# A Mamba block with its convolutions on one core: extras in other state slots, convolutions in five parts, other states' products on GpSimd

## What is computed

```python
x = x + _L0_conv_ref(_gn(x))      # 3x3 dilation (max)
x = x + _L1_conv_ref(_gn(x), ...) # pixel-unshuffle by 4, LayerNorm, Mamba, shuffle back
x = x + _L2_conv_ref(_gn(x), ...) # 3x3 convolution, 8 -> 8 channels
x = x + _L3_conv_ref(_gn(x), ...) # the same with other weights
```

```python
h = h * jnp.exp(dt_t[..., None] * A) + (dt_t * x_t)[..., None] * B_t[:, None, :]
y = jnp.einsum('bds,bs->bd', h, C_t)
```

## Time and profile before

| what | value |
|---|---|
| time, median of 3 runs | 15,045.57 us (15,040.47 to 15,050.49) |
| the profiled execution | 15,054.33 us, its span 15,052.5 us |
| VectorE busy | 13,978.7 us, 93% |
| POOL busy | 13,580.6 us, 90% |
| TensorE busy | 12,595.5 us, 84% |
| ScalarE busy | 8,975.3 us, 60% |
| chain that ended last, by engine | PE 33%, DVE 29%, issue 21%, POOL 9%, ACT 4% |
| TensorE's mean granted clock | 0.949 |

### The profile page before, as it was taken

One profiled execution on the slowest core, in us unless ns is written; L12 is line 12 of the kernel. 1 busy time (PEld: TensorE's weight loads), 2 busy tenths in 40 slices (PEclk: granted clock), 3 DMA queues, 4 the chain that ended last, 5 costly groups with the idle time before them and its releaser, 6 DMA issues.

```text
span 15052.5 us, 162697 instructions
## 1 busy us (share of the span) xinstructions
PE 12595.5 (84%) x27626; PEld 4973.4 (33%) x27626; DVE 13978.7 (93%) x12371; ACT 8975.3 (60%) x16239; POOL 13580.6 (90%) x6103
## 2 busy tenths in 40 slices
PE   4888888888888888888888888888888888888887
PEld 1333333333333333333333333333333333333332
DVE  5999999999999999999999999999999999999995
ACT  3556665566665666665656665666656666666563
POOL 5999999999999999999999999999999999999995
PEclk9999999999999999999999999999999999999998
DMA  3343443434434344443444434344343444434442
GB/s 93 105 118 116 111 123 104 125 108 112 123 106 127 106 111 121 111 124 104 113 121 110 123 106 121 113 112 122 105 129 105 109 123 111 122 107 113 121 109 81
DMA packets 1258399, 1701.57 MB, mean 113 GB/s; under 512 B 402204, under 2 KB 551140, under 8 KB 1257124
## 3 DMA queue, kind: packets, MB, share of 16 engines
q1 hardware_dynamic: 1257220, 1689.56, 40.4%
HBM read 1525.54 MB, written 124.13 MB: 110 GB/s over the span
## 4 chain that ended last, share of the span: by engine, by line
PE 33%; DVE 29%; issue 21%; POOL 9%; ACT 4%; DVEq 1%; DMA 1%; SPq 1%; POOLq 0%; ACTq 0%
PE y_ps L1026 18%; DVE h L1192 16%; DVE u_in L1176 10%; POOL hc L659 7%; PE side_ps L1037 2%; PE side_ps L1041 2%; PE b_ps L1077 2%; PE proj_ps L980 2%; POOL u_in L636 2%; PE y_ps L1023 2%; PE proj_ps L1002 2%; PE side_ps L1012 1%; PE side_ps L1045 1%; DVE vmax L1155 1%; DVE stats L1124 1%
## 5 line engine op out<-in xcount | busy, mean ns | idle before, releaser
L659 POOL TENSOR_TENSOR hc<-h,c_sb 128x1024 f32<-128x1024 f32 x4096 | 9604.5, 2358 | 952.5 <-DVE h L1192 816.6
L1192 DVE TENSOR_TENSOR_SCAN h<-a_ps,carry,u_in 128x512 f32<-128x512 f32 x7168 | 8774.5, 1264 | 367.0 <-ACT a_ps L792 196.1
L1026 PE MATMUL y_ps<-hc,ident 128*128 128x512 f32 x16400 | 8183.7, 629 | 446.3 <-POOL hc L659 440.0
L792 ACT ACTIVATE a_ps<-dt,a_neg 128x512 f32<-128x512 f32 x8192 | 5569.3, 688 | 4634.2 <-DVE h L1192 4604.4
L1026 PEld LDWEIGHTS y_ps<-hc,ident 128*128 128x128 f32 x16400 | 3191.3, 200 | 3985.2 <-issue 3065.3
L1176 DVE TENSOR_TENSOR u_in<-dtx,b_ps 128x1024 f32<-128x1024 f32 x2816 | 3368.2, 1196 | 228.0 <-PE b_ps L1077 186.4
L636 POOL TENSOR_TENSOR u_in<-dtx,b_sb 128x1024 f32<-128x1024 f32 x1281 | 3020.9, 2358 | 0.1
L1077 PE MATMUL b_ps<-b_parts,select 96*128 96x512 bf16 x2816 | 1123.9, 399 | 1639.7 <-DVE u_in L1176 1594.1
L1077 PEld LDWEIGHTS b_ps<-b_parts,select 96*128 96x128 bf16 x2816 | 278.5, 99 | 3169.7 <-DVE u_in L1176 2599.2
L1192 DVE TENSOR_TENSOR_SCAN h<-a_ps,u_in 128x512 f32<-128x512 f32 x1024 | 1202.5, 1204 | 69.0 <-POOL hc L659 55.8
L980 PE MATMUL proj_ps<-u_ln,w_x 128*128 128x512 f32 x2064 | 971.8, 593 | 4.6 <-ACT u_ln L744 3.7
(11 more groups left out here) (100 smaller groups left out, 7224.3 us busy)
## 6 DMA issues: line engine op xcount, KB each, us to landing
c_sb<-bc_dram SPq DMA_DIRECT2D x4100, 256.0 KB, 3.2
b_sb<-bc_dram SPq DMA_DIRECT2D x1283, 256.0 KB, 3.2
raw<-x SPq DMA_DIRECT2D x68, 512.0 KB
x_dram<-vmax SPq DMA_DIRECT2D x68, 512.0 KB, 4.6
z<-x_dram SPq DMA_DIRECT2D x68, 512.0 KB, 8.8
out<-raw SPq DMA_DIRECT2D x272, 128.0 KB
x_dram<-x SPq DMA_DIRECT2D x129, 256.0 KB, 4.0
x<-x_dram SPq DMA_DIRECT2D x136, 224.0 KB, 8.3
```

Of the source, the lines that this page charges most:

```text
L659: pool.tensor_tensor(hc[:, ring_at(c * S + s, HC_RING)], h[:, ring_at(c * S + s, H_RING)], c_sb[:, s // C_GROUP % C_RING, s % C_GROUP:s % ...
L792: act.activation(a_ps[:, a_slot(c * S + s, half)], dt[:, c % 2, half], ACT.Exp, scale=a_neg[:, at:at + 1]).then_inc(a_made, 1)
L1026: mm = pe.matmul(y_ps[:, half], ident[:, :], hc[:, ring_at((c * S + s) % (NC * S), HC_RING), half], start=False, stop=(s == S - 1), skip_g ...
L1192: dve.tensor_tensor_scan(h[:, r, half], a_ps[:, a_slot(c * S + s, half)], u_in[:, s % U_RING, half], start, ALU.mult, ALU.add).then_inc(h_ ...
```

## The change

Ten of the 32 states stay with POOL, but state 22 and 25 go to VectorE, and 0 and 24 to POOL. The last matmul of the output projection moves from slot 5 to slot 8, and ScalarE's copy of it (`RESIDUAL`) from 5 to 7, SP's store with it. ScalarE's copies of the x projection move from slots 6 and 9 to 7 and 10, the Silu block from 13 to 14, the base of the next chunk from 10 to 12, the softplus inputs from 20 and 22 to 21 and 23. Each convolution is issued in five parts instead of four (identity and edge were one part), in the slots of `PLACES`. The group norm "z1" is one slot later.

```diff
-POOL_U = [2, 6, 9, 11, 14, 17, 19, 22, 25, 27]
+POOL_U = [0, 2, 6, 9, 11, 14, 17, 19, 24, 27]
...
-CENTER, VAR, OUT = 0, 3, 5
+CENTER, VAR, OUT = 0, 3, (5, 5, 8)
...
-COPY_X, COPY_Z, SILU = (6, 9), (11, 13), 13
-GATE, STORE_X2, BASE = 2, OUT + 1, 10
+COPY_X, COPY_Z, SILU, RESIDUAL = (7, 10), (11, 13), 14, 7
+GATE, STORE_X2, BASE = 2, RESIDUAL + 1, 12
...
-SPLUS_IN, SOFTPLUS, SUM_DT, DT_X, NEXT_G1 = (20, 22), 23, (23, 24), (25, 27), 30
-PLACES = ((15, 16, 19, 22), (24, 25, 26, 27), (28, 30, S + 2, S + 2))
+SPLUS_IN, SOFTPLUS, SUM_DT, DT_X, NEXT_G1 = (21, 23), 23, (23, 24), (25, 27), 30
+PLACES = ((15, 16, 18, 19, 22), (24, 25, 26, 27, 28), (29, 30, 31, S + 1, S + 2))
...
-MEAN_AT = {"joint": (0, 23), "z1": (3, 29), "x1": (6, 24)}
-VAR_AT = {"joint": (0, 26), "z1": (4, 0), "x1": (6, 27)}
+MEAN_AT = {"joint": (0, 23), "z1": (3, 30), "x1": (6, 24)}
+VAR_AT = {"joint": (0, 26), "z1": (4, 1), "x1": (6, 27)}
...
-    return {"x": TAPS, "conv": 4, "conv_last": 4, "out": NH + 1, "out_last": NH + 1, "xproj": NH}.get(use[0], 1)
+    return {"x": TAPS, "conv": 5, "conv_last": 5, "out": NH + 1, "out_last": NH + 1, "xproj": NH}.get(use[0], 1)
...
-                        if s == OUT:
+                        if s == RESIDUAL:
                             residual(b, ("out", c))
...
-                else:
+                elif part == 3:
                     pe.matmul(side_ps[:, :].rearrange("p (g w q) -> p g w q", g=CB, q=R), ident[:, :],
                               z[:, k * T:(k + 1) * T].rearrange("p (g q w) -> p g w q", g=CB, q=R),
                               start=False, stop=False, skip_group_check=True)
+                else:
                     pe.wait_ge(edge_in[k % 2], b * (NC * 6 * 16) + ((n * NC + k) // 2 + 1) * (6 * 16))
```

More of the change, by code:

```diff
@@ L105, in tensor_extras @@
 def tensor_extras(c, s):
-    at_state = {("center", c): [CENTER], ("var", c): [VAR], ("out", c): [OUT, OUT, OUT], ("xproj", c): XPROJ}
+    at_state = {("center", c): [CENTER], ("var", c): [VAR], ("out", c): OUT, ("xproj", c): XPROJ}
     for half in range(NH):
```

## The result

| what | before | after |
|---|---|---|
| median of 4 runs | 15,048.03 us (15,040.47 to 15,065.19) | 14,821.3 us (14,813.43 to 14,825.65) |
| the profiled execution's span | 15,052.5 us | 14,811.6 us |
| VectorE busy | 13,978.7 us | 13,954.9 us |
| TensorE's mean granted clock | 0.949 | 0.951 |

The ratio is 0.9847 [0.9832, 0.9863]: 1.5% faster, 227 us, or 14.2 us an image, where 1.0% (9.3 us an image) was forecast.

What follows compares the result with a forecast made beforehand. VectorE (95% busy) and POOL (92%) were nearly full, neither bounding alone; VectorE's waits, 47.5 us an image, were what counted. The terms summed to -9.3 us an image, -149 in 16, from 15,045.6 to 14,900 us; range 14,770 to 15,090.

Steps and rivals of the forecast that it cites:

- case A: The forecast itself: every named wait has its cause moved; 14,900 us, with 14,830 to 14,990 for the terms' sizes; chance 0.50.
- case B: Chunk ends cost little: gates wait 2.2 us, clock stays up, moved projection pays; -17.7 us an image, 14,762 us; chance 0.18.
- POOL's waits at 22 and 27: VectorE's waits for POOL at these states, chunks 1 to 4, would go: -11.3 us an image.
- gates, with the clock before them: Six gates behind state 31 would wait 2.6 us each, +10.0 an image, plus 3 x 1.5 us for TensorE's clock.
- image's end, and the program's start: VectorE's wait for the last state's `hc` at an image's end would grow: +3.7 us an image.
- ScalarE: VectorE's waits for ScalarE, at states 15 and 8 among others, would fall from 12.8 to 2.8 us: -10.0 an image.
- broadcasts, with the clock behind the gates: Broadcast wait at state 22 gone, -4.3 us; clock loss behind gates 4 and 7 gone, -1.9; moved projection costed at nothing.
- load of `z`: Loads were costed at nothing: nothing queued on SP would wait longer.
- the lag that it makes at state 31: Time from VectorE's second scan's end to POOL's `hc` start: from 1.4 to 4.8 us, 0.6 more in the last chunks.
- 3 x 1.5 us: TensorE, idle about 2.7 us at the ends into chunks 1, 4, 7, would lose clock speed before y(31), 1.5 us each.
- C's mechanism: Slower: TensorE's clock falls at chunk ends, 1.5 us each; ten falls beyond those counted give 15,137 us; chance 0.17.
- Case D: No difference: POOL waits 1.8, not 0.6 us, for slot 23's logarithm, reaching gate or image's end; 15,050 us; chance 0.10.

Runs made afterwards that it cites:

- last-but-one run: The changed kernel with the statistics of `z` a slot later and the output projection as before: 14,809.87 us, against 14,752.03 with the projection moved.
- the best list: The changed kernel with later `z` statistics and POOL's states 2, 6, 9, 11, 13, 15, 17, 19, 24, 27: 14,644.17 us, against 14,782.03 with the states of before.

## Why the prediction was right in sign and range, and too small in size

The sign and the range (14,770 to 15,090) held, and the time is between the two faster cases: 9 us under the low end of case A (14,830), 59 over case B (14,762). Measured, an image, from the profiled executions:

| term | forecast | measured |
|---|---|---|
| POOL's waits at 22 and 27 | -11.3 | -11.2 (11.3 to 0.1) |
| gates, with the clock before them | +14.5 | +7.7 (5.9 to 13.6) |
| image's end, and the program's start | +3.7 | +3.4 (5.0 to 8.4) |
| ScalarE | -10.0 | -8.6 (12.6 to 4.0) |
| broadcasts, with the clock behind the gates | -6.2 | -8.1 (11.7 to 3.6) |
| load of `z` | 0 | +3.2 |
| other waits | 0 | +0.3 |
| gaps of VectorE under 0.15 us | 0 | -0.2 |
| VectorE's busy time | 0 | -1.5 |
| sum | -9.3 | -15.1 |

The two profiled executions differ by 241 us, 15.1 an image, the medians by 14.2. The forecast had VectorE's own work the same. Its count is, but its busy time fell by 23.8 us in all (13,978.7 to 13,954.9); why was not found.

**POOL at 22 and 27** was right in place and size. So was the lag that it makes at state 31: forecast 4.8 to 5.4, measured 4.2 to 5.3 in seven of eight chunks, and 2.1 in chunk 5, where the statistics give POOL time. The gate behind it costs 0.5 where I had nothing.

**The gates** were sized too high, and this is the term that is furthest off: 13.6 us for the 20.1 that its own waits (15.6) and the clock (4.5) come to. Both halves were too high by about the same.

The half of the lags: with the clock up the six gates cost 2.0 us each on average, not 2.6. Of this the forecast's own sum explains a part. Its terms give 4.8 + 4.4 - 7.05 = 2.15 us, and 2.75 with the later softplus, not "up to 3.0"; four and two of these are 14.1 us, not 15.6.

The half of the clock: "3 x 1.5 us" is 1.4 measured, as the cost of the falls just before y(31). At the ends into chunks 1 and 7 TensorE stands idle before y(31) for 2.4 us, not 2.7, and in the 16 images the clock fell at 5 and at 8 of these ends. Here it fell (the fifth image), the four instructions took 3.68 us, and the granted clock of 3941.9 to 3945.3 was 0.52:

```profile
3941.89 3.68 PE L1026 MATMUL y_ps<-hc,ident 128*128 128x512 f32 x4 [2.41 <-POOL hc L659]
...
3941.90:3945.30 3.40, 3.40 (x4) 1.40 (x5) 1.28 (x1) 0.82 (x2) 3.40 (x2) 0.52 0.27 89
```

and here, in the eighth, it did not after the same idle time, and they took 1.98:

```profile
6646.33 1.98 PE L1026 MATMUL y_ps<-hc,ident 128*128 128x512 f32 x4 [2.42 <-POOL hc L659]
```

At the end into chunk 4 the clock fell in all 16 images, but not at the same place. In six it fell in y(31), after the same 2.41 us. In ten it had fallen before, around an idle time of 3.0 us in which TensorE waits for the statistics of the group norm "z1", and then it stood idle for less or not at all before y(31). Here is such an image, the eighth; eight instructions took 6.20 us, where they took 3.60 in the tenth image:

```profile
6973.84 0.58 PE L951 MATMUL side_ps<-mv,group_z 128*128 128x1 f32 x2 [3.03 <-DVE mv L1142]
...
6974.67 6.20 PE L1026 MATMUL y_ps<-hc,ident 128*128 128x512 f32 x8
```

The earlier fall is cheap. From state 28 to state 12 of the next chunk VectorE needs 59.2 us with it and 60.9 with the fall in y(31). At the ends into 1 and 7 a fall makes the gates 1.4 and 0.8 us longer.

So case B's "the clock stays up" was right in the larger part of the ends into 1 and 7. C's mechanism exists, but costs little: the mean clock is 0.951 for 0.949. The Trainium skill ("TensorE: Matmul & The Clock Gate", HAM oscillation) tells of a clock that falls again and again at idle gaps between bursts; the falls here are of that kind. It does not decide the time of this change.

**ScalarE.** The Silu block's term came out (7.9 us at state 15 to 1.1 at 16), and the run of ScalarE's slots alone gives 9.5 us an image for the 10.0 forecast. State 8 keeps 1.45 us of its 3.5, and state 25 costs 1.4, hardly more than its 1.2 before. These three make the 4.0 us that remain, where I left 2.8. The Trainium skill ("ScalarE: Activation LUTs", What ACT_TABLE_LOAD costs) has a drain beside the load; as in the earlier trace rows none is seen here, and the decay starts 0.01 us behind the load.

**Broadcasts.** "I cost it at nothing" for the moved projection was wrong: 44 us alone and 52 to 58 in the last-but-one run, 2.7 and 3.3 to 3.6 us an image, which is about the bound that the text named and gave to case B. My reason for nothing was that what is spared at state 7 would be asked for at state 10. It is asked for there, but only 0.8 us an image of it. And what the forecast calls the broadcast's wait at state 22 is the one in slot 22, for the product of state 23.

**Loads.** "cost nothing" was false in its reasoning. I looked at `b_sb` and `c_sb` and at the edge loads, but not at what waits for the store that I had listed as moved. The store, the reload of `z` and the statistics are a chain through DRAM, and its slack before was below the 6.8 us that the last load moved. The later statistics took it out (69 us).

**Case D** did not come: it needed 1.2 us more lag at each end than forecast, and the lags at state 31 lie within the forecast or below.

**Case B** was nearer in its mechanism than the forecast: gates of 2.0 us (it had 2.2), the clock mostly up, and the moved projection paying. With the `z` wait out of the way the kernel takes 14,752 us, 10 under B's value. That it comes so near is in part luck, since ScalarE gave 1.4 us an image less than counted and VectorE's busy time fell by 1.5.

The forecast was 79 us too high. The gates (6.8 us an image), the broadcasts (1.9) and VectorE's busy time (1.5) made it too pessimistic. ScalarE (1.4) and the `z` wait (3.2), which no case had, took a part of that back. That the time came within the range is owed in part to errors of opposite sign.

## What to carry to other kernels

With in-order engines and short rings, count for each engine how far it lags at the places where someone needs its last result (here the gate and the image's end): moving work from a stall to such a place trades one wait for another. Spreading it gained over four times as much (138 us from the best list over the old one, for 30). For every store that moves, follow the data to its reload and to the first reader. Judge parts of a schedule in company, since what one part frees the next bottleneck can take: the same list cost 58 us alone and in the whole gained 17, which is not told from nothing.

## What the runs showed of the hardware that was not expected

- The releaser that the profile names is the one whose event came last by its clock, and where two come close together it can be the wrong one: VectorE starts 0.33 to 0.36 us after the end of the `hc` that frees its buffer, and for the same wait of 1.45 to 1.47 us at state 22 one run names POOL and another ScalarE.
- After the same idle time of 2.40 to 2.42 us TensorE's clock fell in some images and not in others (13 of 32 ends into chunks 1 and 7). At the end into chunk 4 it fell in every image, in ten of them around an earlier idle time of 3.0 us. What decides was not found.
- VectorE's product `u_in` kept its time in the whole run (1194 ns mean, 1196 before) while POOL was busy 92% of the time beside it. One of its two inputs, `b_ps`, lies in PSUM, so this says nothing of a product with both in SBUF.
